# A two-layer transformer kernel: four buffers of expert weights and one shared normalised tile in layer 1, and the router's steps spread over more tiles

## What is computed

```python
h = layernorm(x) * (1 + ca) + sa
x = x + ga * gated_attention(h)          # 16 heads of width 8, softmax(q k^T / sqrt(8) + relative bias)
h = layernorm(x) * (1 + cb) + sb
# the feed-forward: a causal attention of low rank, then a mixture of experts
h = h + mla(rmsnorm(h, g1), Wq, Wdkv, Wuk, Wuv, Wo)
t = rmsnorm(h, g2).reshape(B * S, D)
logits = t @ gate_w                       # (tokens, 8)
top_v, top_i = top_k(logits, 2)
gates = softmax(top_v)
combine = zeros(tokens, 8).at[arange, top_i].add(gates)
hid = silu(einsum('td,edh->teh', t, w1))  # 8 experts, 128 x 256
ye = einsum('teh,ehd->ted', hid, w2)
h = h + einsum('te,ted->td', combine, ye)
x = x + gb * h
```

## Time and profile before

| | us |
|---|---|
| median of 3 executions | 2079.36 |
| lowest and highest | 2076.03, 2079.79 |
| the profiled execution's own time | 2073.5 |
| its span, first to last instruction | 2071.5 |
| PE busy in it | 1779.4 (86%) |
| DVE, ACT, POOL busy | 1444.1, 1015.6, 857.9 |
| granted PE clock, mean | 0.943 of full speed |

### The profile page before, as it was taken

One profiled execution on the slowest core, in us unless ns is written; L12 is line 12 of the kernel. 1 busy time (PEld: TensorE's weight loads), 2 busy tenths in 40 slices (PEclk: granted clock), 3 DMA queues, 4 the chain that ended last, 5 costly groups with the idle time before them and its releaser, 6 DMA issues.

```text
span 2071.5 us, 56863 instructions
## 1 busy us (share of the span) xinstructions
PE 1779.4 (86%) x21284; PEld 1306.9 (63%) x21284; DVE 1444.1 (70%) x4537; ACT 1015.6 (49%) x1992; POOL 857.9 (41%) x1253
## 2 busy tenths in 40 slices
PE   4485898898875729999999999999999999999997
PEld 2374677677763517766667666667666667766665
DVE  4574778876761127777787786787886887778765
ACT  1252544455441206666655654654654555655542
POOL 3500101110013017767655654655754663664530
PEclk7797999999996959999999999999999999999998
DMA  2512211222006411012013012012012112111211
GB/s 94 166 24 72 76 42 51 61 75 74 7 6 208 142 67 39 33 57 77 17 71 96 11 69 87 21 72 86 26 66 85 32 60 83 35 54 40 83 32 48
DMA packets 102694, 131.72 MB, mean 64 GB/s; under 512 B 14448, under 2 KB 87536, under 8 KB 101272
## 3 DMA queue, kind: packets, MB, share of 16 engines
q1 hardware_dynamic: 70600, 98.59, 14.6%
q10 hardware_dynamic: 28496, 18.10, 3.0%
q0 software_dynamic: 3328, 11.40, 1.7%
HBM read 100.05 MB, written 28.15 MB: 62 GB/s over the span
## 4 chain that ended last, share of the span: by engine, by line
PE 45%; DVE 8%; issue 6%; DMA 5%; POOL 2%; ACT 1%; ACTq 1%; SPq 1%; POOLq 0%; DVEq 0%
PE ps L1737 13%; PE ps L1752 7%; PE ps L1723 6%; PE ps L1846 5%; PE ps L1832 4%; DMA l_w_e<-in_L_ffn_w_dram 2%; DVE l_X L1900 2%; DMA l_stack<-parts_dram 2%; PE ps L1199 1%; POOL l_Y L1583 1%; PE ps L1208 1%; PE ps L1762 1%; PE ps L1783 1%; DVE l_xn L1931 1%; ACT PT L1625 1%
## 5 line engine op out<-in xcount | busy, mean ns | idle before, releaser
L1583 POOL TENSOR_SCALAR l_Y<-l_X,l_nmax 128x512 f32<-128x512 f32 (+3 forms) x1024 | 674.6, 664 | 521.1 <-PE ps L1737 286.0
L1625 ACT ACTIVATE PT<-ps 128x512 f32<-128x512 f32 (+3 forms) x1024 | 520.0, 517 | 405.8 <-PE ps L1737 356.3
L1737 PE MATMUL ps<-ident,l_Y 128*128 128x128 f32 x3328 | 549.7, 280 | 11.7 <-ACT PT L1625 7.7
L1737 PEld LDWEIGHTS ps<-ident,l_Y 128*128 128x128 f32 x3328 | 387.2, 142 | 195.3 <-issue 82.4
L1900 DVE CUSTOM_DVE_ANT_0 l_X<-ps,strips 128x512 f32<-128x512 f32 x512 | 342.1, 687 | 134.2 <-PE ps L1723 130.9
L1723 PE MATMUL ps<-l_stack 72*128 72x512 bf16 (+3 forms) x1024 | 351.0, 345 | 66.9 <-DVE l_nmax L1900 50.0
L1900 DVE CUSTOM_DVE_ANT_0 l_X<-ps,mask 128x384 f32<-128x384 f32 (+3 forms) x512 | 238.5, 485 | 41.0 <-PE ps L1723 35.6
L1752 PE MATMUL ps<-PT,v_aug 128*10 128x128 f32 x6656 | 230.1, 274 | 0.0
L1752 PEld LDWEIGHTS ps<-PT,v_aug 128*10 128x10 f32 x6656 | 156.8, 91 | 71.5 <-ACT PT L1625 42.6
L1723 PEld LDWEIGHTS ps<-l_stack 72*128 72x128 bf16 x1024 | 102.0, 100 | 102.6 <-DVE l_nmax L1900 77.3
L1832 PE MATMUL ps<-l_fT,l_w_e 128*128 128x512 f32 x256 | 138.9, 631 | 12.1 <-DMA l_w_e<-in_L_ffn_w_dram 9.3
(11 more groups left out here) (276 smaller groups left out, 2508.6 us busy)
## 6 DMA issues: line engine op xcount, KB each, us to landing
stack<-parts_dram SPq DMA_DIRECT2D x48, 384.0 KB
l_stack<-parts_dram SPq DMA_DIRECT2D x64, 288.0 KB
l_stack<-parts_dram SPq DMA_DIRECT2D x192, 96.0 KB
l_w_e<-in_L_ffn_w_dram ACTq DMA_DIRECT2D x128, 128.0 KB, 2.2
parts_dram<-l_parts SPq DMA_DIRECT2D x32, 384.0 KB, 2.5
strips<-bias_dram POOLq DMA_DIRECT2D x16, 448.0 KB, 11.2
parts_dram<-parts SPq DMA_DIRECT2D x16, 384.0 KB, 10.9
w_e<-in_L_ffn_w_dram SPq DMA_DIRECT2D x12, 256.0 KB, 5.7
```

What stands on the lines that cost most here:

```text
L1583: nc.gpsimd.tensor_scalar(Y[:, n % Y_BUFS, 0:w], X[:, n % X_BUFS, 0:w], -1.0, nmax[:, n % 8:n % 8 + 1], ALU.mult, ALU.add).then_inc(y_pool, 1)
L1625: nc.scalar.activation(dst, src, ACT.Exp).then_inc(moved, 1)
L1737: last = nc.tensor.transpose(ps[:, to, k * P:(k + 1) * P], Y[:, n % Y_BUFS, k * P:(k + 1) * P], ident[:])
```

## The change

Three edits:

- `W_BUFS` is 4. The load issued after the output of expert n is that of expert n + 4, and four pairs are issued at the start of layer 1. The number of semaphores `experts_loaded` follows.
- The tile `xf` is gone; the scaled input of the experts is written to `xn`. Ahead of each write to `xn` DVE waits until PE has transposed what stood there before (`xn_read`).
- In `STAGES`, `top0` is cut into `top0` (3 instructions, step 15) and `rank0` (4, step 16), `top1` into `top1` (3, step 17) and `rank1` (3, step 18), `gap` goes from 18 to 19, and `combine` is cut into `combine` (3, step 20) and `halve` (4, step 21). In `LAST_STAGES` the halves keep the old steps.

```diff
-STAGES = dict(wo=1, add=3, square=4, power=5, scale=7, turn=10, logits=12, read=14, top0=15, top1=16, gap=18,
-              combine=20, first=12, each=6, second=2, tanh=1, mul=2, ye=9, half=2, sum=2)
+STAGES = dict(wo=1, add=3, square=4, power=5, scale=7, turn=10, logits=12, read=14, top0=15, rank0=16, top1=17, rank1=18, gap=19,
+              combine=20, halve=21, first=12, each=6, second=2, tanh=1, mul=2, ye=9, half=2, sum=2)
...
-X_BUFS, Y_BUFS, PT_BUFS, W_BUFS, VW = 3, 4, 2, 3, HD + 2
+X_BUFS, Y_BUFS, PT_BUFS, W_BUFS, VW = 3, 4, 2, 4, HD + 2
...
+XN_TURNS = [what for what in SLOT if what[0] in ("xp", "xm", "xf")]
...
-        xf = sb("l1_xf", [P, TT, C])
...
-                        src = xf if name == "xf" else xn
                         for t in range(TT):
-                            last = nc.tensor.transpose(ps[:, to, t * P:(t + 1) * P], src[:, t, :], ident[:])
+                            last = nc.tensor.transpose(ps[:, to, t * P:(t + 1) * P], xn[:, t, :], ident[:])
...
+                def xn_read(what):
+
+                    before = XN_TURNS[XN_TURNS.index(what) - 1] if what != XN_TURNS[0] else None
+                    if before is not None:
+                        dve.wait_ge(turned, SLOT[before] + 1)
+
                 def normalised(n, b):
                     dve.wait_ge(rstd_ready[n], b + 1)
+                    xn_read(("xp" if n == 0 else "xm", b))
...
-                        nc.vector.tensor_tensor(xf[:], h, bc(rstd[3][:].unsqueeze(2), wide), ALU.mult).then_inc(tok_ready[2], 1)
+                        xn_read(("xf", b))
+                        nc.vector.tensor_tensor(xn[:], h, bc(rstd[3][:].unsqueeze(2), wide), ALU.mult).then_inc(tok_ready[2], 1)
```

More of the change, by code:

```diff
@@ L1257 @@
 HALVES = 2
-STAGES = dict(wo=1, add=3, square=4, power=5, scale=7, turn=10, logits=12, read=14, top0=15, top1=16, gap=18,
-              combine=20, first=12, each=6, second=2, tanh=1, mul=2, ye=9, half=2, sum=2)
-LAST_STAGES = dict(wo=0, add=1, square=2, power=3, scale=4, turn=5, logits=7, read=8, top0=10, top1=10, gap=11,
-                   combine=12, first=8, each=2, second=0, tanh=1, mul=1, ye=3, half=0, sum=2)
+STAGES = dict(wo=1, add=3, square=4, power=5, scale=7, turn=10, logits=12, read=14, top0=15, rank0=16, top1=17, rank1=18, gap=19,
+              combine=20, halve=21, first=12, each=6, second=2, tanh=1, mul=2, ye=9, half=2, sum=2)
+LAST_STAGES = dict(wo=0, add=1, square=2, power=3, scale=4, turn=5, logits=7, read=8, top0=10, rank0=10, top1=10, rank1=10, gap=11,
+                   combine=12, halve=12, first=8, each=2, second=0, tanh=1, mul=1, ye=3, half=0, sum=2)
 def stages(b):
@@ L2044, in moe @@
                     for n in range(2):
-                        if i != p[f"top{n}"]:
-                            continue
-                        linked()
-                        link(nc.vector.tensor_reduce(tops[:, n], logit[:], AX.X, ALU.max))
-                        linked()
-                        link(nc.vector.tensor_tensor(small[:, n], logit[:], bc(tops[:, n].unsqueeze(2), few), ALU.is_equal))
-                        linked()
-                        link(nc.vector.tensor_tensor(small[:, n], small[:, n], bc(rank[:].unsqueeze(1), few), ALU.mult))
+                        if i == p[f"top{n}"]:
+                            linked()
+                            link(nc.vector.tensor_reduce(tops[:, n], logit[:], AX.X, ALU.max))
+                            linked()
+                            link(nc.vector.tensor_tensor(small[:, n], logit[:], bc(tops[:, n].unsqueeze(2), few), ALU.is_equal))
+                            linked()
+                            link(nc.vector.tensor_tensor(small[:, n], small[:, n], bc(rank[:].unsqueeze(1), few), ALU.mult))
+                        if i != p[f"rank{n}"]:
+                            continue
                         linked()
@@ L2071, in moe @@
                         link(nc.vector.tensor_tensor(tops[:, 5], tops[:, 4], tops[:, 2], ALU.mult))
+                    if i == p["halve"]:
                         linked()
```

## The result

| | before | after |
|---|---|---|
| median of 6 executions each, us | 2077.15 (2071.38 to 2079.79) | 2055.91 (2053.63 to 2057.64) |
| ratio, with its 95% interval | | 0.9901 [0.9884, 0.9918] |
| the profiled execution's own time, us | 2073.5 | 2056.3 |
| its span, us | 2071.5 | 2054.3 |
| PE busy, us | 1779.4 | 1771.5 |

The changed kernel is 21.2 us faster in the medians and 17.2 us in the two profiled spans. The prediction said 2059.6 us.

The account below looks back on a forecast made before the run. PE, with its waits and clock, was taken to bound layer 1. Loads 12.5, router 3.9 and clock falls 3.4 summed to 19.8 us, off the median 2079.36: 2059.6 us; range 2048 to 2070.6, chance 0.84.

Follow-up runs that it names:

- e3_share: The kernel before with only the shared tile: `xf` gone, DVE waits ahead of writes to `xn`, three buffers, router steps unmoved; 2072.28 us, ratio 0.9996.
- e4_late_loads: The changed kernel with four buffers, but each load of weights issued one expert later, when three buffers allowed it; 2065.75 us, ratio 0.9974.
- e6_late_combine: The changed kernel with `gap` at step 20 instead of 19 and both parts of `combine` at step 22 instead of 20 and 21; 2050.61 us, ratio 0.9883.
- the early gap: The changed kernel with `gap` at step 18 instead of 19, `rank1` staying behind the shift of tile 12; 2059.88 us, ratio 0.9930.

## What to carry to other kernels

A transfer that is needed soon and runs beside a large one has to be issued earlier by the worst landing, not the median one; a further buffer is only the means, and filling it late gives nothing. Before adding one, look which of several loads on one semaphore is late, and whether the waiting instruction reads it. When a wait for one engine's long run of small instructions is cut by spreading them, look at which engine waits for the last of them and what is queued behind it there: one step of `gap` was worth 0.6 us a batch, and another 0.6 came only when the DVE work ahead of the next bound moved as well. One profiled execution shows the falls of the clock that it happened to have; compare several before a sum of passes is taken for the price of a change.

## What the runs showed that was not expected

- The clock falls in some executions and not in others behind the same wait of PE, and the length of the wait does not decide it. Behind the router's 1.6 us it fell in 8 of 24 batches. Behind the wait of 1.57 us that stands seven times in every execution outside the router it fell in 3 of 91 (e3_share, e4_late_loads, e6_late_combine). Behind 20 waits for weights it fell three times, after 1.83, 1.97 and 2.47 us, and not after the longest of all, 2.99 us in e4_late_loads. Its row and window:

```profile
1106.49 1.12 PE L1831 MATMUL ps<-l_fT,l_w_e 128*128 128x512 f32 x2 [2.99 <-DMA l_w_e<-in_L_ffn_w_dram]
```

```profile
1105.00:1110.00 5.00, 3.51 (x18) 2.33 (x19) 1.72 (x4) 1.76 (x4) 1.26 (x3) 1.00 0.31 107
```

- A fall in the router or in a gated pass costs 1.3 to 1.7 us. Behind the waits of 1.19 to 1.44 us of the early gap, one in each of six batches, none was seen.
- Removing three quarters of the stacks' bytes made the third pass 1.0 us shorter too (56.9 to 55.9 us) and took the longest landing of the weights from 9.5 to 4.7 us, the median staying at 2.2. Of the two loads of a pair, 128 KB each and issued 0.4 us apart, the stacks hit w2 (up to 9.5 us) far more than w1 (up to 3.5); what in the two transfers makes the difference stays open.
- Without a wait the distance of the two loads comes back as 7.71 us again and again, in three of five batches of the changed kernel and of the small stacks; the others lie between 7.98 and 8.49. Where it falls, a neighbour may move the other way (7.87 to 8.31 us behind the one of batch 1 that fell to 7.71).
